# Eight slots for the experts' results, expert weights stored by blocks, and x turned earlier

## The chip, the cores and the metric

The kernel runs on one core of a Trainium2 chip. The metric is device time in microseconds, the median of several executions. TensorE (PE) multiplies, VectorE (DVE), ScalarE (ACT) and GpSimd (POOL) do the rest, SyncE (SP) mostly issues DMAs.

## What is computed

Four batches of 512 rows of 512 numbers pass through linear cross-attention over 1024 context rows and then a mixture of eight experts, two for each row. Cut to what matters:

```python
# x = x + attention(layernorm(x), ctx)
q = feature_map(query @ Wq.T);  gate = sigmoid(query @ Wg.T + bg)
k, v = split(kv @ Wkv.T);       k = feature_map(k)          # 16 heads of 32
attn = (q @ (k.T @ v)) / (q @ k.sum() + EPS)                # per head
out = (attn * gate) @ Wo.T
# x = x + ffn(layernorm(x))
w, sel = top_k(x @ Wr, 2);      w = softmax(w)
out = sum over the two chosen experts e of w_e * (x @ We[e] + be[e])
```

All products are of float32 accuracy. They are made of three products of fp32r halves: each operand is split in an upper half and the rest (high and low in the code), and high x high, high x low, low x high are summed.

## The kernel before

**Attention** goes batch by batch. `keys(b)` takes the eight context tiles: transpose (T c), K product, V product, and the kv sum (KV) of the tile before; between them stand the routing of the batch before (T z, L, K) and the transposes of this batch's x (T x 0 to 3). The order is written out by hand in the list KEYS, and every engine walks the same list with its own part: for a transpose TensorE turns the tile into PSUM, ACT copies the upper half (line 611), DVE subtracts to get the lower half (line 781). After V, ACT copies the product to SBUF (line 654), and KV of that tile waits for it. `queries(b)` follows: Q, gates, attention, output product, and the residual x2, which lies in the buffer `gate` (x2 is the same memory) and is stored to the output by SP (`store_x2`).

**Expert weights** are split on POOL beside attention: `cut_to_dram(e, h)` splits half an expert (lines 503 and 505) and stores both halves to the HBM buffer `we_halves` in one DMA (line 509). An expert's copy in SBUF needs the memory of attention's weights (R), so SP loads it back, 2 MB at once (`load_halves`, line 365), as these come free in the last batch: experts 1 to 3 during its keys and queries, 4 and 5 after the gates, 6 and 7 after the last output product. POOL issues in order; between the cuts it also makes rstd and shift of the layer norms (`scale`, lines 469 and 470), for which ACT waits, and scatters the normed rows into the experts' regions of the HBM buffer `xs` (line 462). At the start it fills the heads of these regions with zeros, in as many DMAs as there are result slots (YS).

**The expert stage** works on tiles of 128 rows of one expert, 39 in all: 17 with the full tiles of the first three batches, which begin while the last batch is routed, then 22 for the rest. Four of these 22 are empty here. For each tile m: `load_tile` brings the rows; TensorE turns them (line 1188), ACT and DVE split them (lines 698 and 785); TensorE multiplies (lines 1121 to 1123); ACT writes the expert's bias times the row's weight into the result slot `y_sb[m % YS]` (line 724) and first waits until the add of tile m - YS, which used this slot, has landed; DVE adds the weighted product to it (line 1072); POOL adds the result's rows to the output in HBM by an indirect accumulating DMA (`add_rows`, line 579). Two adds that may meet in a row of the output must not be in flight together. Two tiles of one expert have no row in common. So the first tile of an expert waits for the landing of the add just before it where their rows may meet (`tile_alone`), and the first and second tile wait for all older ones still in flight (`tile_early`); a third tile waits for nothing. At tile 17 (M0) all adds before have to be down. With YS slots, up to YS - 1 adds can be older and in flight, and the code names each of them:

```python
elif m >= 1:
    alone = pool.value_load(tile_alone[0:1, m:m + 1], ...)
    early_ = pool.value_load(tile_early[0:1, m:m + 1], ...)
    pool.wait_ge(added[(m - 1) % YS], alone + 16 * ((m - 1) // YS + 1))
    for d in range(2, min(m, YS - 1) + 1):
        pool.wait_ge(added[(m - d) % YS], early_ + 16 * ((m - d) // YS + 1))
```

The first tile of the stage is turned at 390.7 us, between the last output products. Which expert has how many tiles follows from the inputs; in the order of tiles it is 3, 2, 3, 2, 2, 2, 3 (experts 0 to 6), the four empty ones, then 1, 2, 2, 3, 2, 3, 2, 3 (experts 0 to 7).

Of the kernel before, what the change touches and what calls it, by code (L numbers as in the profile page):

```python
# [5 lines left out]
F32 = mybir.dt.float32  # L6
# [8 lines left out]
P = 128  # L15
# [5 lines left out]
def xattn_moe_kernel(nc, x, ctx_in, wq_t, wg_t, bg, wkv_t, wo_t, wr, we, be, out):  # L21
# [34 lines left out]
    XS, YS = 4, 4  # L56

    xs_dram = nc.dram_tensor("xs", [(E + 1) * ROWS, W], F32, kind="Internal").ap()
    wx_dram = nc.dram_tensor("we_halves", [E, P, 2 * KT * D], F32, kind="Internal").ap()
# [3 lines left out]
    with ExitStack() as stack:  # L63
# [43 lines left out]
        y_sb = [khat[:, 0, :], khat[:, 1, :], expk[:, 0, :], expk[:, 1, :]]  # L107
# [7 lines left out]
        x2 = gate  # L115
        w_raw += [gate[:, :, :], qhat[:, :, :], w_raw[0]]
# [25 lines left out]
        gap = sb("gap", [P, 1])  # L142
        egap = sb("egap", [P, 1])
        total = sb("total", [P, 1])
# [12 lines left out]
        w_sel = sb("w_sel", [P, 2 * YS])  # L157
        out_idx = sb("out_idx", [P, 2 * YS], U32)
# [37 lines left out]
        e_high, we_ready = sem("e_high"), sem("we_ready")  # L196
# [109 lines left out]
        def _(sp):  # L306
# [64 lines left out]
            sp.wait_ge(wx_stored, 16 * 2 * (E - 1))  # L371
# [14 lines left out]
            load_halves(7)  # L386
# [12 lines left out]
        def _(pool):  # L399
# [96 lines left out]
            def cut_to_dram(e, h):  # L496
# [4 lines left out]
                pool.wait_ge(wx_stored, 16 * u)  # L501
# [7 lines left out]
                pool.dma_start(wx_dram[bass.ds(e, 1), :, :].rearrange("x p (a k d) -> p (x a) k d", a=2, k=KT)[:, :, ks, :],  # L509
                               aux[:, :, :].rearrange("p (a k) d -> p a k d", a=2).bitcast(F32)).then_inc(wx_stored, 16)  # L510
# [50 lines left out]
            def add_rows(m):  # L561
# [17 lines left out]
                nc.gpsimd.indirect_dma_start(out=out_rows[:, :], out_offset=bass.IndirectOffsetOnAxis(ap=out_idx[:, m % (2 * YS):m % (2 * YS) + 1], axis=0),  # L579
# [12 lines left out]
        def _(act):  # L592
# [100 lines left out]
            def high_m(m, slot):  # L693
                act.wait_ge(MOE["t_m"], mth(m))
                if m == 0:
                    act.wait_ge(wx_stored, 16 * 2 * (E - 1))
# [16 lines left out]
            def gate_bias(m):  # L713
# [581 lines left out]
```

## Time and profile before

| | us |
|---|---|
| median of 3 runs | 560.09 (558.15 to 564.46) |
| the profiled execution | 555.62 |
| its span in the trace | 554.1 |
| TensorE busy | 517.2 (93%) |
| DVE / ACT / POOL busy | 304.5 / 208.8 / 203.4 |

Attention takes the first 390 us, the expert stage the rest. A trace row has a start, a duration, the engine (SPq, ACTq, POOLq: its instruction queue), the line, the tiles (out<-in), and in brackets how long the engine was idle before and what ended that. TensorE's granted clock is 0.993 of full over the span.

### The profile page before, as it was taken

To read this page: it belongs to the slowest core of one execution; us is meant where nothing else is said; L and a number is where in the kernel's file an instruction comes from. 1 tells how busy PE (TensorE), PEld (TensorE's weight loads), DVE (VectorE), ACT (ScalarE), POOL (GpSimd) and SP (SyncE) were. 2 spreads that over 40 slices of the span, in tenths; PEclk is the share of its full clock that TensorE was granted. 3 is DMA by queue.
4 is the path that set the end of the run, shared out by engine and by line. 5 is a ranking of instruction groups with operands and counts; after the bars stand their busy time and mean duration, and the time that the engine had idled before them with its cause. 6 is when DMAs were issued, how large, how long until landed. Compare 5 with 4: busy or idle time off the path is not lost.

```text
span 554.1 us, 12191 instructions
## 1 busy us (share of the span) xinstructions
PE 517.2 (93%) x4080; PEld 420.1 (76%) x4080; DVE 304.5 (55%) x918; ACT 208.8 (38%) x372; POOL 203.4 (37%) x221
## 2 busy tenths in 40 slices
PE   6999999999999999999999999999988878997990
PEld 4777788788878888777888877788866666886880
DVE  4483248547524764753585475378577674453540
ACT  6455432443443234344324344432343233332430
POOL 4443246502654040364404036100133563444453
PEclk9999999999999999999999999999999999999997
DMA  8922943652445135244513412697998788746855
GB/s 254 401 86 75 294 152 115 231 188 72 149 167 188 41 126 180 78 152 159 182 46 129 176 55 105 228 351 277 342 334 190 177 161 166 155 96 121 166 73 68
DMA packets 34361, 92.93 MB, mean 168 GB/s; under 512 B 4544, under 2 KB 4544, under 8 KB 33280
## 3 DMA queue, kind: packets, MB, share of 16 engines
q0 software_dynamic: 14960, 42.56, 28.9%
q1 hardware_dynamic: 18048, 47.22, 24.9%
q10 hardware_dynamic: 1296, 2.40, 1.3%
q8 instruction: 35, 0.57, 0.4%
q14 instruction: 22, 0.18, 0.1%
HBM read 53.81 MB, written 40.18 MB: 170 GB/s over the span
## 4 chain that ended last, share of the span: by engine, by line
PE 58%; DMA 14%; issue 6%; POOL 3%; POOLq 3%; DVE 2%; ACT 1%; ACTq 1%; DVEq 0%
PE pj L1121 16%; PE pj L1123 16%; PE pj L1122 16%; DMA out_dram<-khat,out_idx 6%; DMA out_dram<-buf,out_idx 5%; PE tp L1113 5%; PE pj L1208 2%; POOL aux L505 1%; PE kvb L1180 1%; DMA wraw<-in_L_ffn_We_dram 1%; DMA we_halves<-aux 1%; POOLq L574 1%; PE pj L1130 1%; POOLq L573 1%; PE tp L1188 1%
## 5 line engine op out<-in xcount | busy, mean ns | idle before, releaser
L1121 PE MATMUL pj<-R 128*128 128x512 f32 x448 | 184.2, 411 | 5.7 <-DVE R L781 5.0
L1123 PE MATMUL pj<-R 128*128 128x512 f32 x448 | 176.2, 393 | 0.0
L1122 PE MATMUL pj<-R 128*128 128x512 f32 x448 | 175.4, 392 | 0.0
L1121 PEld LDWEIGHTS pj<-R 128*128 128x128 f32 x448 | 84.7, 189 | 23.2 <-DVE R L781 7.3
L1123 PEld LDWEIGHTS pj<-R 128*128 128x128 f32 x448 | 84.5, 189 | 19.0
L1122 PEld LDWEIGHTS pj<-R 128*128 128x128 f32 x448 | 84.9, 189 | 15.1
L1121 PE MATMUL pj<-R,aux 128*128 x156 | 64.8, 416 | 12.0 <-DVE aux L785 10.2
L1123 PE MATMUL pj<-R,aux 128*128 x156 | 61.4, 393 | 0.0
L1122 PE MATMUL pj<-R,aux 128*128 x156 | 60.8, 390 | 0.0
L781 DVE TENSOR_TENSOR R<-tp,R 128x512 fp32r<-128x512 f32 x64 | 43.8, 684 | 23.2 <-ACT R L611 23.2
L846 DVE SCALAR_TENSOR_TENSOR khat<-buf,khat 128x512 f32<-128x512 f32 x32 | 24.2, 756 | 51.6 <-ACT buf L650 50.9
L469 POOL TENSOR_TENSOR rstd<-rstd,mhalf 128x1 f32<-128x1 f32 (+1 forms) x20 | 13.4, 670 | 100.4 <-DVE rstd L799 100.3
L579 POOL DMA_INDIRECT out_dram<-khat,out_idx x20 | 31.4, 1571 | 39.9 <-issue 15.2
L1121 PEld LDWEIGHTS pj<-R,aux 128*128 128x128 f32 x156 | 29.3, 188 | 19.9 <-issue 15.0
L579 POOL DMA_INDIRECT out_dram<-buf,out_idx x19 | 29.6, 1560 | 39.7 <-DMA out_dram<-khat,out_idx 13.6
L611 ACT CAST R<-tp 128x512 fp32r<-128x512 f32 x64 | 37.6, 588 | 16.9 <-PE tp L1113 16.6
L462 POOL DMA_INDIRECT xs<-normed,xidx x16 | 18.5, 1155 | 67.2 <-DVE xidx L832 64.1
L654 ACT COPY buf<-pj 128x512 f32<-128x512 f32 x32 | 18.8, 587 | 51.3 <-PE pj L1123 51.3
L647 ACT ACTIVATE khat<-pj 128x512 f32<-128x512 f32 x32 | 19.1, 597 | 47.6 <-PE pj L1123 47.6
L505 POOL TENSOR_TENSOR aux<-wraw,aux 128x1024 fp32r<-128x1024 f32 x14 | 35.8, 2554 | 1.2
L1123 PEld LDWEIGHTS pj<-R,aux 128*128 128x128 f32 x156 | 29.3, 188 | 6.5
L1122 PEld LDWEIGHTS pj<-R,aux 128*128 128x128 f32 x156 | 29.4, 188 | 5.1
(196 smaller groups left out, 699.2 us busy)
## 6 DMA issues: line engine op xcount, KB each, us to landing
we_halves<-aux POOLq DMA_DIRECT2D x14, 1024.0 KB, 4.9
R<-we_halves SPq DMA_DIRECT2D x7, 2048.0 KB, 9.5
buf<-xs SPq DMA_DIRECT2D x34, 264.0 KB, 3.7
buf<-in_ctx_dram SPq DMA_DIRECT2D x15, 512.0 KB, 3.6
wraw<-in_L_ffn_We_dram POOLq DMA_DIRECT2D x14, 512.0 KB, 6.6
wraw<-in_x_dram SPq DMA_DIRECT2D x4, 1024.0 KB, 8.8
out_dram<-gate SPq DMA_DIRECT2D x4, 1024.0 KB, 5.2
xs<-zeros POOLq DMA_DIRECT2D x4, 594.0 KB, 9.7
```

The lines of the kernel that those rows point to most:

```text
L462: nc.gpsimd.indirect_dma_start(out=xs_dram[:, :], out_offset=bass.IndirectOffsetOnAxis(ap=xidx[:, t, j:j + 1], axis=0), in_=rows[t], in_of ...
L505: nc.gpsimd.tensor_tensor(aux[:, 2:4, :], e_raw[:, ks, :], aux[:, 0:2, :].bitcast(F32), ALU.subtract).then_inc(wx_low, 1)
L579: nc.gpsimd.indirect_dma_start(out=out_rows[:, :], out_offset=bass.IndirectOffsetOnAxis(ap=out_idx[:, m % (2 * YS):m % (2 * YS) + 1], axis=0),
L611: nc.scalar.copy(dst, src).then_inc(SEMS["h_" + kind], 1)
L647: nc.scalar.activation(khat[:, i % 2, :], pj_bank("expk", i)[:, :], ACT.Relu)
L654: nc.scalar.copy(vones[:, i % 2, :, 0:HD], pj_bank("v_copied", i)[:, :].rearrange("p (g c) -> p g c", g=HEADS)).then_inc(SEMS["v_copied"], 1)
L781: nc.vector.tensor_tensor(lo, tp_bank("l_" + kind, i)[:, :, :], hi.bitcast(F32), ALU.subtract).then_inc(SEMS["l_" + kind], 1)
L846: nc.vector.scalar_tensor_tensor(khat[:, i % 2, :], expk[:, i % 2, :], 1.0, khat[:, i % 2, :], ALU.min, ALU.add).then_inc(SEMS["khat"], 1)
L1113: last = nc.tensor.transpose(bank[:, k, :], src[:, k * P:(k + 1) * P], ident[:, :])
L1121: nc.tensor.matmul(bank[:, :], s_hi(k), m_hi(k), start=(k == 0), stop=False)
L1122: nc.tensor.matmul(bank[:, :], s_hi(k), m_lo(k), start=False, stop=False)
L1123: last = nc.tensor.matmul(bank[:, :], s_lo(k), m_hi(k), start=False, stop=(k == KT - 1))
```

## The change

- YS goes from 4 to 8. The four new slots are the four tiles of x2 (the buffer `gate`); ACT waits for the store of the last batch's x2 before it writes the first of them (tile 4). The rings of weights and indices have YS + 2 = 10 columns in place of 2 YS = 8.
- `we_halves` has the shape [expert, 8 blocks, partition, 512] in place of [expert, partition, 8 x 512]. A store of halves becomes two DMAs, a load reads eight pieces of 2 KB for each partition in place of one of 16 KB.
- Expert 7 is loaded in two halves: the first right after expert 3's load, the second after expert 6's.
- In KEYS the transpose of x's tile 3 (T x 3) goes from behind V of the last context tile to ahead of it.
- TensorE starts with a product on zeros (128 columns) and makes another (256 columns) after its first transposes.
- gap, egap and total share one tile.

```diff
-    XS, YS = 4, 4
+    XS, YS = 4, 8
-    wx_dram = nc.dram_tensor("we_halves", [E, P, 2 * KT * D], F32, kind="Internal").ap()
+    wx_dram = nc.dram_tensor("we_halves", [E, 2 * KT, P, D], F32, kind="Internal").ap()
-        y_sb = [khat[:, 0, :], khat[:, 1, :], expk[:, 0, :], expk[:, 1, :]]
+        y_sb = [khat[:, 0, :], khat[:, 1, :], expk[:, 0, :], expk[:, 1, :]] + [x2[:, t, :] for t in range(TT)]
...
-            KEYS += [("P", "k", i), ("T", "c", i + 1) if i + 1 < ST else ("T", "x", 2), ("P", "v", i)]
+            KEYS += [("P", "k", i)]
+            KEYS += [("T", "c", i + 1)] if i + 1 < ST else [("T", "x", 2), ("T", "x", 3)]
+            KEYS += [("P", "v", i)]
...
-            KEYS += [("T", "x", 3)] if i == ST - 1 else []
...
             def load_halves(e):
-                sp.wait_ge(wx_stored, 16 * 2 * e)
+                sp.wait_ge(wx_stored, 32 * 2 * e)
                 sp.wait_ge(we_ready, 16 * e)
-                sp.dma_start(R[:, 2 * e:2 * e + 2, :, :].rearrange("p a k d -> p (a k d)").bitcast(F32), wx_dram[e, :, :]).then_inc(we_ready, 16)
+                sp.dma_start(R[:, 2 * e:2 * e + 2, :, :].rearrange("p a k d -> p (a k) d").bitcast(F32),
+                             wx_dram[e, :, :, :].rearrange("a p d -> p a d")).then_inc(we_ready, 16)
+
+            def load_half(e, a):
+                if a:
+                    sp.wait_ge(we_ready, 16 * e)
+                    sp.wait_ge(half_loaded, 16)
+                sp.dma_start(R[:, 2 * e + a, :, :].bitcast(F32),
+                             wx_dram[e, a * KT:(a + 1) * KT, :, :].rearrange("k p d -> p k d")).then_inc(we_ready if a else half_loaded, 16)
...
             load_halves(3)
+            load_half(7, 0)
...
             load_halves(6)
-            load_halves(7)
+            load_half(7, 1)
...
-                pool.dma_start(wx_dram[bass.ds(e, 1), :, :].rearrange("x p (a k d) -> p (x a) k d", a=2, k=KT)[:, :, ks, :],
-                               aux[:, :, :].rearrange("p (a k) d -> p a k d", a=2).bitcast(F32)).then_inc(wx_stored, 16)
+                for a in range(2):
+                    pool.dma_start(wx_dram[bass.ds(e, 1), a * KT + 2 * h:a * KT + 2 * h + 2, :, :].rearrange("x k p d -> p (x k) d"),
+                                   aux[:, 2 * a:2 * a + 2, :].bitcast(F32)).then_inc(wx_stored, 16)
...
                 act.wait_ge(paid, m + 1)
+                if m == YS - TT:
+                    act.wait_ge(x2_stored, 16 * B + 16)
                 if m >= YS:
                     act.wait_ge(added[m % YS], 16 * (m // YS + 1))
...
-            pe.wait_ge(pool_step, 3)
...
+            def idle_product(n):
+                nc.tensor.matmul(kvb[1][:, 0:n], zeros[:, 0:P], zeros[:, 0:n], start=True, stop=True)
+
+            pe.wait_ge(zeroed, 1)
+            idle_product(P)
+            pe.wait_ge(pool_step, 3)
             pe.wait_ge(ctx_first, 16)
             turn("c", 0, 0, ctx_raw[:, 0, 0, :])
+            idle_product(D // 2)
```

## Rows read from the trace of the kernel before

**Rows 1.** The page, busy time of the engines over the whole span.

```profile
PE 517.2 (93%) x4080; PEld 420.1 (76%) x4080; DVE 304.5 (55%) x918; ACT 208.8 (38%) x372; POOL 203.4 (37%) x221
```

**Rows 2.** Table by windows: window, length, busy (instructions) by engine, clock, DMA, GB/s.

```profile
161.00:258.00 97.00, 95.98 (x864) 78.72 (x864) 53.42 (x168) 37.09 (x68) 33.19 (x34) 1.00 0.38 133
...
422.00:554.10 132.10, 108.01 (x536) 87.03 (x536) 63.49 (x200) 40.40 (x66) 64.08 (x44) 0.97 0.69 133
```

**Rows 3.** Chain of waits, 396 us to the end: shares; start, us, what.

```profile
by line: DMA out_dram<-khat,out_idx 21.1%; DMA out_dram<-buf,out_idx 19.3%; issue 11.7%; PE pj L1121 6.8%; PE pj L1123 6.5%; PE pj L1122 6.3%; POOLq L574 3.3%; POOLq L573 2.8%; PE tp L1188 2.5%; POOL out_dram L579 1.9%; DVE buf L1072 1.4%; 
...
455.99 4.86 DMA out_dram<-buf,out_idx
461.10 0.51 issue
```

**Rows 4.** Waits of ACT from 400 us, of TensorE 430 to 535: us, times, longest.

```profile
ACT khat L724 <- DMA out_dram<-khat,out_idx: 30.9, 12, 5.1
ACT buf L724 <- DMA out_dram<-buf,out_idx: 28.9, 13, 4.6
...
PE pj L1121 <- DVE aux L785: 10.2, 8, 2.4
```

**Rows 5.** POOL's adds, line 579: timeline, then what ended its idle time.

```profile
422.20 1.55 POOL L579 DMA_INDIRECT out_dram<-buf,out_idx  x1 [9.70 <-DVE xidx L832]
...
461.81 1.55 POOL L579 DMA_INDIRECT out_dram<-khat,out_idx  x1 [4.26 <-DMA out_dram<-buf,out_idx]
...
546.44 1.55 POOL L579 DMA_INDIRECT out_dram<-buf,out_idx  x1 [0.92 <-DMA out_dram<-khat,out_idx]
...
  DMA out_dram<-khat,out_idx: 21.0, 8
  DMA out_dram<-buf,out_idx: 19.3, 8
```

**Rows 6.** Timeline of DVE: the results of tiles 2, 3 and 38.

```profile
408.08 0.75 DVE L1072 SCALAR_TENSOR_TENSOR buf<-pj,w_sel,buf 128x512 f32<-128x512 f32 x1 [0.91 <-ACT buf L724]
412.21 0.75 DVE L1072 SCALAR_TENSOR_TENSOR buf<-pj,w_sel,buf 128x512 f32<-128x512 f32 x1 [0.26 <-PE pj L1123]
...
542.06 0.75 DVE L1072 SCALAR_TENSOR_TENSOR buf<-pj,w_sel,buf 128x512 f32<-128x512 f32 x1 [3.12 <-ACT buf L724]
```

**Rows 7.** DMA issues 396 to 422, then 470 to 530: count, KB, us to landing.

```profile
R<-we_halves SPq DMA_DIRECT2D x2, 2048.0 KB, 11.2
out_dram<-khat,out_idx POOLq DMA_INDIRECT x2, 9.7
out_dram<-buf,out_idx POOLq DMA_INDIRECT x1, 10.3
...
out_dram<-buf,out_idx POOLq DMA_INDIRECT x10, 4.8
```

**Rows 8.** The same: stores of halves 105 to 119 us, then of the page.

```profile
we_halves<-aux POOLq DMA_DIRECT2D x1, 1024.0 KB, 6.4
...
we_halves<-aux POOLq DMA_DIRECT2D x14, 1024.0 KB, 4.9
```

**Rows 9.** Timeline of POOL in batch 0.

```profile
52.22 2.48 POOL L529 DMA_DIRECT2D xs<-zeros  x4
...
87.44 0.68 POOL L509 DMA_DIRECT2D we_halves<-aux  x1 [0.81 <-POOL aux L505]
```

**Rows 10.** Timeline of ACT and TensorE at batch 0's output products.

```profile
99.07 0.82 ACT L621 ACTIVATE normed<-gate,shift,rstd 128x512 f32<-128x512 f32 x1 [4.92 <-POOL shift L470]
...
101.14 0.50 PE L1121 MATMUL pj<-R 128*128 128x512 f32 x1 [0.51 <-DVE R L781]
```

**Rows 11.** Timeline at the end of a batch's keys.

```profile
256.08 0.60 PE L1113 MATMUL tp<-ident,num 128*128 128x128 f32 x4
256.28 0.59 ACT L654 COPY buf<-pj 128x512 f32<-128x512 f32 x1 [1.63 <-PE pj L1123]
...
258.14 0.50 PE L1121 MATMUL pj<-R 128*128 128x512 f32 x1 [0.66 <-DVE R L781]
```

**Rows 12.** Timeline of TensorE at the start, first K product of context tile 1.

```profile
14.96 0.50 PE L1121 MATMUL pj<-R 128*128 128x512 f32 x1 [0.50 <-DVE R L781]
```

More of the change, by code:

```diff
@@ L141, in xattn_moe_kernel @@
         top = sb("top", [P, E])
-        gap = sb("gap", [P, 1])
-        egap = sb("egap", [P, 1])
-        total = sb("total", [P, 1])
+        odds = sb("odds", [P, 3])
+        gap, egap, total = [odds[:, i:i + 1] for i in range(3)]
         idx8 = sb("idx8", [P, E], U32)
@@ L156, in xattn_moe_kernel @@
         xidx = sb("xidx", [P, TT, 2], U32)
-        w_sel = sb("w_sel", [P, 2 * YS])
-        out_idx = sb("out_idx", [P, 2 * YS], U32)
+        w_sel = sb("w_sel", [P, YS + 2])
+        out_idx = sb("out_idx", [P, YS + 2], U32)
         used = sb("used", [P, 1 + E])
@@ L195, in xattn_moe_kernel @@
         w_high, w_low = sem("w_high"), sem("w_low")
-        e_high, we_ready = sem("e_high"), sem("we_ready")
+        e_high, we_ready, half_loaded = sem("e_high"), sem("we_ready"), sem("half_loaded")
         first_loaded = [sem(f"first_loaded{k}") for k in range(KT)]
@@ L370, in _ @@
             load_halves(2)
-            sp.wait_ge(wx_stored, 16 * 2 * (E - 1))
+            sp.wait_ge(wx_stored, 32 * 2 * (E - 1))
             sp.dma_start(be_all[:, 0:4, :], be[0:4, :].rearrange("(a e) d -> a e d", a=1).broadcast_to((P, 4, D))).then_inc(be_loaded, 16)
@@ L500, in cut_to_dram @@
                 pool.wait_ge(e_loaded[h], 16 * e)
-                pool.wait_ge(wx_stored, 16 * u)
+                pool.wait_ge(wx_stored, 32 * u)
                 passed()
@@ L578, in add_rows @@
                 passed()
-                nc.gpsimd.indirect_dma_start(out=out_rows[:, :], out_offset=bass.IndirectOffsetOnAxis(ap=out_idx[:, m % (2 * YS):m % (2 * YS) + 1], axis=0),
+                nc.gpsimd.indirect_dma_start(out=out_rows[:, :], out_offset=bass.IndirectOffsetOnAxis(ap=out_idx[:, m % (YS + 2):m % (YS + 2) + 1], axis=0),
                                              in_=y_sb[slot], in_offset=None, bounds_check=B * L - 1, oob_is_err=False, compute_op=ALU.add).then_inc(added[slot], 16)
@@ L695, in high_m @@
                 if m == 0:
-                    act.wait_ge(wx_stored, 16 * 2 * (E - 1))
+                    act.wait_ge(wx_stored, 32 * 2 * (E - 1))
                 act.wait_ge(MOE["m_done"], mth(m - 2))
@@ L724, in gate_bias @@
                 nc.scalar.activation(y_sb[m % YS], be_all[:, bass.ds(e, 1), :].rearrange("p a d -> p (a d)"), ACT.Identity,
-                                     scale=w_sel[:, m % (2 * YS):m % (2 * YS) + 1]).then_inc(bias_gated, 1)
+                                     scale=w_sel[:, m % (YS + 2):m % (YS + 2) + 1]).then_inc(bias_gated, 1)
             bias_in(TT - 1)
@@ L919, in pay @@
                 e = dve.value_load(tile_expert[0:1, m:m + 1], min_val=0, max_val=E - 1)
-                n = m % (2 * YS)
+                n = m % (YS + 2)
                 row = xs_raw[:, m % XS, :]
@@ L1071, in copy_y @@
                 dve.wait_ge(bias_gated, m + 1)
-                nc.vector.scalar_tensor_tensor(y_sb[m % YS], pj[m % 2][:, :], w_sel[:, m % (2 * YS):m % (2 * YS) + 1], y_sb[m % YS],
+                nc.vector.scalar_tensor_tensor(y_sb[m % YS], pj[m % 2][:, :], w_sel[:, m % (YS + 2):m % (YS + 2) + 1], y_sb[m % YS],
                                                ALU.mult, ALU.add).then_inc(MOE["y_copied"], 1)
```

## The prediction

> **What bounds the kernel now.** The page comes first: TensorE is busy 93% of the span [rows 1]. That says "TensorE-bound", and it is an average over two unlike stages. The table by windows separates them [rows 2]: from 161 to 258 us TensorE is busy 95.98 of 97 us, but from 422 us to the end only 108.01 of 132.10 us. So the first 390 us, attention, go at TensorE's pace, and the last 132 us need another reason.
>
> The chain of waits of the last stretch names it [rows 3]: 40% of that stretch is the landing of two kinds of transfer, the accumulating stores `out_dram<-khat` and `out_dram<-buf`, the adds of line 579. ACT's waits seem to tell why: line 724, which prepares a result slot, waited 30.9 + 28.9 us for such landings [rows 4], since slot m % 4 is free only when add m-4 has landed. TensorE idles behind it, 10.2 us in 8 waits after 430 us [rows 4]. That is the wait which eight slots take away.
>
> But does the end hang on it? For that one compares when a result is there (end of DVE line 1072) with when its add starts on POOL. Result 3 is complete at 412.21 + 0.75 = 412.96 us [rows 6] and its add starts at 422.20 [rows 5]. Result 38, the last: 542.06 + 0.75 = 542.81 [rows 6] against 546.44 [rows 5]. Over the 36 adds from the fourth on, of which these are the first and the last, I find a finished result that waited 3.6 to 13.1 us for its add. The adds never wait for results; they wait for each other: the first tile of an expert waits until the previous expert's last add landed (line 575), the second until all older ones have (line 577). The rows show it: the add of 461.81 starts 0.96 us after the landing of the add of 455.99 (455.99 + 4.86 = 460.85) [rows 3, 5], and the next of the same expert follows as soon as POOL has issued this one, 1.55 us [rows 5] and 0.35 more. So from 422.20 us to the end the adds are a closed chain, through landings of about 5 us and issues, and TensorE, ACT and DVE run beside it with 3.6 us in hand or more.
>
> **Part 1, eight slots.** ACT's 59.8 us of waiting for landings goes, TensorE catches up its 10.2 us of idle time [rows 4], and the last product ends some 10 us earlier. None of it is on the adds' chain: which add waits for which is set by the experts' borders, and these stay. Worth to the end: 0. What is late next is the adds' chain, as before. What the part does put on that chain: an add now names up to seven earlier slots instead of three. The wait that ends last comes first in the list, so the four more stand behind it. From that landing (460.85) to the last sequencer instruction ahead of the start (461.10) pass 0.25 us for three instructions [rows 3], 0.08 us each. Four more waits are two instructions if two waits share one (0.16 us), four if not (0.33 us). The answer on line 579 names 8 + 8 adds that a landing released [rows 5]; with four more whose gap is put down otherwise I count 20 links. I take 0.15 us: 20 x 0.15 = +3.0 us; bounds 0 (hidden) and 20 x 0.33 = +6.6. The other adds have these waits under the 1.55 us of the issue before. The first zero fill is cut into eight stores instead of four, counted in part 3. Slots 4 to 7 lie in x2, whose store is issued before the first add and takes some 6 us; the first result that goes there is number 4, after 412.96, so that wait costs 0.
>
> **Part 2, the halves in HBM by blocks.** An expert's 2 MB load was 16 KB in one piece for each partition; now it is eight rows of 2 KB. The first half of expert 7 goes ahead of the last batch's queries, so 1 MB less lies behind expert 6's load. The place where this meets the end is the head of the chain: between 396 and 422 us two such loads take 11.2 us each and the adds beside them 9.7 and 10.3 us [rows 7], while in the quiet stretch from 470 us an add lands in 4.8 us [rows 7]. Add 3 starts at 422.20 [rows 5] because add 2 landed only after these 10.3 us. What would an add take beside 2 KB pieces? The nearest row is the 1 MB store at 111.9 us, beside x and context loads whose rows are 2 KB: 6.4 us, against 4.9 alone [rows 8], 1.5 more. So 4.9 + 1.5 = 6.4 us for add 2, and the chain starts 10.3 - 6.4 = 3.9 us sooner. Value -3.9; bounds 0 (no relief) and -5.5 (4.8 us, as in quiet). Result 3 (412.96) and the scatter's inputs are there in time, so the gain isn't stopped on the way. Everything behind it moves with it. The loads themselves grow a little; expert 6 is due first at tile 14, at about 449 us, and is there by some 410 to 420: hidden, and even 15 us a load would be.
>
> **Part 3, each store of halves in two.** 14 stores of 1 MB become 28 of 0.5 MB, all on POOL; one issue takes 0.68 us there, 0.61 until the next begins [rows 9]. In batches 1 to 3 POOL waits for DVE (up to 36.9 us at line 469), so they are hidden. In batch 0 they aren't: POOL's work from 52 to 99 us is one chain, the rstd at its end comes late, ACT waited 4.92 us for it and TensorE then 0.51 us at 101.14 [rows 10]. On that path lie: the second issue after the store of 74.78, ahead of the loads of 75.70 (+0.6); the landing of the store of 87.44 before the copy of 92.45 (+0.25 to 0.6); the second issue before rstd at 98.08 (+0.6); and four more zero fills of 0.62 us each (52.22, 2.48 us for four [rows 9]), which stand ahead of a store that waits for the fills' traffic anyway until 70.2 us, +0 to 0.6. Together 1.5 to 2.4: value +1.8 us, and TensorE has no later slack in this stage to win it back. Bounds +0.9 and +2.5.
>
> I take the two halves' fixed parts to run side by side; the third rival has them one behind the other. The Trainium skill (DMA: Bandwidth & Descriptors, section "Anatomy of one DMA — SWDGE (gpsimd) path") gives a GpSimd DMA about 2.0 us that don't shrink with its size, which speaks against cutting one in two. The 4.9 us of [rows 8] for 1 MB agree with such a part; whether two of them overlap, no row here shows.
>
> **Part 4, x's fourth tile turned before the last V product.** At the end of each batch's keys TensorE waits for x's last lower half: 0.66 us at 258.14 [rows 11], and 0.66 to 0.71 in the other batches. Moved ahead, its copies run under the V product. But its 0.44 us of transposes also covered ACT's copy of V: that copy starts at 256.28 and takes 0.59, ends 256.87 [rows 11], and would now come 0.79 us after V's end with only 0.37 us of kv work in between: a new gap of 0.42 us before the last kv sum. Per batch 258.14 - 256.08 = 2.06 us before, 0.79 + 0.03 + 0.43 + 0.44 = 1.69 after: -0.37, four times -1.5 us. Bounds 0 and -2.7 (the gaps whole).
>
> **Part 5, idle products at the start.** The first products go at half the pace of the later ones. Two products on zeros could bring the clock up earlier. But TensorE then waits 0.50 us at 14.96 for DVE [rows 12], which follows ACT's copies of the weights, and these follow their DMA. Faster products only make that wait longer: 0. They run while TensorE waits for its first inputs: cost 0.
>
> The merged small tiles and the shorter ring of ten columns add no instruction: 0.
>
> **Sum.** +3.0 - 3.9 + 1.8 - 1.5 = -0.6 us. The profiled execution took 555.62 us (span 554.1), so 555.0 in its terms; the median of the runs shown is 560.09, 4.5 higher, so 559.5.
>
> **Rivals.**
> - *No relief at the head (0.15)*: adds are slow there because of all the bytes, not the pieces: -0.6 + 3.9 = +3.3, 563.4 us. For: DMA is also busy with 2 KB and 2112-byte rows; against: 6.4 us in [rows 8] under like load.
> - *Full relief (0.15)*: adds 1 and 2 also start 0.9 us after their results (result 2: 408.08 + 0.75 [rows 6]): 408.83 + 0.9 + 4.8 + 0.95 = 415.5, 6.7 us sooner: -3.4, 556.7 us.
> - *Fixed parts in series (0.08)*: 1 MB takes 2.6 us at the 401 GB/s of the page's busiest slice, so of a store's 4.9 us [rows 8] 2.3 aren't data. Twice on batch 0's path that is 4.6 in place of 0.3: +4.3, together +3.7: 563.8 us. Against: POOL issues the second half 0.6 us behind the first and waits for neither.
> - *The slots pay in full (0.07)*: the end follows TensorE, 10.2 us less: 549.3. For: the page's 93% and ACT's waits. Against: results that lie finished for 3.6 us and more.
> - *Slower (0.07)*: the waits' list. If every extra wait also takes its own register work, 0.16 us each, a link costs 0.64 and 20 links 12.8: 0.3 - 3.9 + 12.8 = +9.2, 569 us. It decides from 0.46 us a link. Against: 0.08 us an instruction in [rows 3].
> - My forecast holds the rest, 0.48, with -4 to +3 us.
>
> **How the numbers follow.** Within 1% (5.6 us), about what can be told from no change, lie the forecast, no relief, the series and most of full relief. Faster by over 1%: the slots in full 0.07, and 0.08 from full relief together with hidden waits. Slower: the list 0.07, and 0.04 where no relief meets the upper bound of the waits. The range runs from full relief with its lower bounds (553) to no relief with costly waits (565).
>
> **What would show it.** In the new profile: ACT's waits for `out_dram` landings nearly gone; TensorE's last product about 10 us earlier in the stretch, with the end of the kernel not following; results finished over 10 us before their adds at the end; add 2 landing in 6 to 7 us and the fourth add near 418 us; the start 1.1 instead of 0.95 us behind a landing; TensorE's wait near 101 us grown to about 2.3; no wait on line 781 at the keys' ends and a new one of 0.4 before kv. I am wrong if the end moves with TensorE, or if the adds' landings in the quiet stretch change.

## The result, and the profile after

| | us |
|---|---|
| changed kernel, median of 4 | 565.74 (561.69 to 569.73) |
| kernel before, on the same chip | 559.12 (556.54 to 564.46) |
| ratio | 1.0099, interval 1.0059 to 1.0139 |
| again, median of 6, beside 11 of the kernel before | 565.59; ratio 1.0122 (1.0084 to 1.0160) |

The forecast was 559.5 us, within 553 to 565. The kernel became slower by 1%: 5.5 us by the first ratio, 6.8 by the second. Its profiled execution has a span of 565.0 us against 554.1, which is 2.0% and more than either ratio. So not all that the two traces differ in is the change, and the experiments have to say what is.

**Where the slots were to help, they did what they do.** First the waits of ACT at the slots (line 737 now) from 400 us: of the 59.8 us of [rows 4] for landings nothing is left here (a second profile of the changed kernel has 13.7 us, behind results that lie still further ahead).

```profile
ACT khat L737 <- issue: 3.4, 4, 2.2
ACT buf L737 <- DVE out_idx L937: 1.9, 2, 1.3
ACT gate L737 <- issue: 1.5, 4, 0.7
```

Then the ends of DVE and of POOL in the timeline. The last result is complete at 544.96 + 0.75 = 545.71 us and its add starts 11.65 us later; in [rows 5, 6] it was 3.63. The adds still follow each other's landings.

```profile
544.96 0.75 DVE L1085 SCALAR_TENSOR_TENSOR gate<-pj,w_sel,gate 128x512 f32<-128x512 f32 x1 [1.97 <-PE pj L1135]
...
552.12 1.55 POOL L590 DMA_INDIRECT out_dram<-gate,out_idx  x1 [2.09 <-DMA out_dram<-buf,out_idx]
...
557.36 1.55 POOL L590 DMA_INDIRECT out_dram<-gate,out_idx  x1 [1.11 <-DMA out_dram<-gate,out_idx]
```

**The head of the chain.** Adds 2 and 3 in POOL's timeline. In the trace add 2 lands 6.53 us after its start, at 425.42 (10.3 us in [rows 7]), and add 3 follows it by 1.03 us. Attention ended 8.4 us later than before, add 3 starts only 4.25 us later than the 422.20 of [rows 5].

```profile
418.89 1.56 POOL L590 DMA_INDIRECT out_dram<-buf,out_idx  x1 [2.76 <-issue]
426.45 1.55 POOL L590 DMA_INDIRECT out_dram<-buf,out_idx  x1 [6.01 <-issue]
```

**The new stall lies in batch 0.** Where TensorE waited 0.51 us [rows 10], it now waits 5.61, because ACT waited 9.63 us for POOL's shift (4.92 before), which POOL makes right behind a late rstd:

```profile
103.72 0.59 POOL L479 TENSOR_TENSOR rstd<-rstd,mhalf 128x1 f32<-128x1 f32 x1
104.62 0.81 ACT L632 ACTIVATE normed<-gate,shift,rstd 128x512 f32<-128x512 f32 x1 [9.63 <-POOL shift L480]
...
106.68 0.79 PE L1133 MATMUL pj<-R 128*128 128x512 f32 x1 [5.61 <-DVE R L794]
```

and the granted clock of TensorE falls during that wait, at 103.5 us, and is back at 110.3. The line of the page gives it in tenths for 40 slices of 14 us; the eighth, 99 to 113 us, is the one. First the kernel before:

```profile
PEclk9999999999999999999999999999999999999997
```

then the changed one, and below it its table by windows (window, length, busy by engine, clock, DMA share, GB/s). Half clock is the lower of the two levels, 1.2 of 2.4 GHz. The kernel before has 1.00 in both windows.

```profile
PEclk9999999799999999999999999999999899999985
```

```profile
99.00:104.00 5.00, 2.07 (x12) 1.50 (x10) 0.40 (x3) 0.00 (x0) 4.24 (x5) 0.95 0.24 92
104.00:110.00 6.00, 3.32 (x8) 2.64 (x9) 2.98 (x7) 2.92 (x5) 1.97 (x6) 0.50 0.59 186
```

Following POOL back from there one comes to the first store of expert halves. POOL's timeline before, after the fills of [rows 9]:

```profile
59.19 0.72 POOL L509 DMA_DIRECT2D we_halves<-aux  x1 [0.64 <-POOL aux L505]
70.34 1.03 POOL L503 CAST aux<-wraw 128x1024 fp32r<-128x1024 f32 x1 [10.43 <-issue]
...
74.78 0.68 POOL L509 DMA_DIRECT2D we_halves<-aux  x1 [0.60 <-POOL aux L505]
```

and after:

```profile
53.38 4.38 POOL L540 DMA_DIRECT2D xs<-zeros  x8
57.76 1.06 POOL L513 CAST aux<-wraw 128x1024 fp32r<-128x1024 f32 x1
...
61.92 1.50 POOL L520 DMA_DIRECT2D we_halves<-aux  x2 [0.63 <-POOL aux L515]
75.44 1.04 POOL L513 CAST aux<-wraw 128x1024 fp32r<-128x1024 f32 x1 [12.02 <-issue]
79.55 0.73 POOL L520 DMA_DIRECT2D we_halves<-aux  x1 [0.59 <-POOL aux L515]
```

The second cut begins when the first store has landed: at 75.44 instead of 70.34 us. These 5.1 us are nearly all of the 5.6 us by which rstd is late at 103.72 (98.08 before).

**Keys.** The new order shows as forecast: no wait of 0.66 us behind the kv sums, but one of 0.38 ahead of the last (0.42 forecast).

```profile
264.95 0.59 ACT L665 COPY buf<-pj 128x512 f32<-128x512 f32 x1 [1.58 <-PE pj L1135]
...
265.68 0.46 PE L1192 MATMUL kvb<-buf,khat 128*32 128x33 f32 x32 [0.38 <-ACT buf L665]
```

**Two more differences, and a suspicion.** In the middle of the keys of batches 1 to 3 TensorE now has a wait that the trace of the kernel before doesn't have, and the whole batch gets some 0.7 us longer by what stands around it:

```profile
236.50 0.50 PE L1192 MATMUL kvb<-buf,khat 128*32 128x33 f32 x25 [0.47 <-issue]
```

And at 432.73 us DVE had stood still for 3.46 us before it took logits whose product was done at 428.75. The results of tiles 6 to 9 come late after it, and the adds 9 to 11 start 2.4 to 3.0 us behind their results: for these three the results are the bound. From add 8 to add 12 pass 18.3 us here and 15.2 in the mean of the other profiles: about 3 us of the end.

```profile
432.73 0.17 DVE L817 COPY lg<-pj 128x8 f32<-128x8 f32 x1 [3.46 <-remote]
...
456.18 1.58 POOL L590 DMA_INDIRECT out_dram<-khat,out_idx  x1 [3.99 <-DMA out_dram<-khat,out_idx]
```

At the start the first profile of the changed kernel differs too: its keys of batch 0 end 1.6 us later than before.

The theory at this point: the two stores or the eight fills make batch 0 late (one had been priced, +1.8 us for both), the list of waits is dearer than 3.0 us, and the last two differences may be of one execution only. The rival: eight slots themselves disturb the early tiles.

### The profile page after: what moved, and what is told of

The parts are those of the page before. It is cut to its first block, busy times and chain, and to the rows that moved or that the text cites. A ratio compares the mean times of both kernels' runs of the same rounds, so it can differ in the third digit from the quotient of the medians.

```text
span 565.0 us, 12322 instructions
## 1 busy us (share of the span) xinstructions
PE 522.4 (92%) x4084; PEld 423.2 (75%) x4084; DVE 307.2 (54%) x918; ACT 211.4 (37%) x372; POOL 214.2 (38%) x239
## 4 chain that ended last, share of the span: by engine, by line
PE 73%; DMA 5%; issue 4%; POOL 2%; DVE 2%; another core or an unknown queue 1%; POOLq 1%; ACT 0%; DVEq 0%
PE pj L1133 21%; PE pj L1135 20%; PE pj L1134 19%; PE tp L1125 5%; PE tp L1200 3%; PE pj L1220 2%; PE kvb L1192 2%; POOL aux L515 1%; DMA wraw<-in_L_ffn_We_dram 1%; PE pj L1142 1%; DMA we_halves<-aux 1%; DMA out_dram<-khat,out_idx 1%; DMA out_dram<-buf,out_idx 1%; DMA out_dram<-gate,out_idx 1%
## 5 line engine op out<-in xcount | busy, mean ns | idle before, releaser
L1134 PEld LDWEIGHTS pj<-R 128*128 128x128 f32 x448 | 85.5, 191 | 15.3
L479 POOL TENSOR_TENSOR rstd<-rstd,mhalf 128x1 f32<-128x1 f32 (+1 forms) x20 | 13.3, 666 | 100.4 <-DVE rstd L812 100.3
L709 ACT CAST aux<-tp 128x512 fp32r<-128x512 f32 x39 | 22.8, 584 | 60.3 <-PE tp L1200 52.2
L590 POOL DMA_INDIRECT out_dram<-gate,out_idx x19 | 29.7, 1565 | 37.5 <-issue 24.5
L472 POOL DMA_INDIRECT xs<-normed,xidx x16 | 17.1, 1068 | 64.8 <-DVE xidx L845 61.8
L1133 PEld LDWEIGHTS pj<-R,aux 128*128 128x128 f32 x156 | 29.7, 190 | 15.3 <-issue 10.2
L1135 PEld LDWEIGHTS pj<-R,aux 128*128 128x128 f32 x156 | 29.5, 189 | 6.7
L916 DVE SCALAR_TENSOR_TENSOR qhat<-buf,qhat 128x512 f32<-128x512 f32 x16 | 17.4, 1086 | 30.9 <-ACT buf L690 30.8
```

What stands on the lines that cost most here:

```text
L709: nc.scalar.copy(xsT_hi[:, slot, :, :], tp[slot][:, :, :]).then_inc(MOE["h_m"], 1)
L1133: nc.tensor.matmul(bank[:, :], s_hi(k), m_hi(k), start=(k == 0), stop=False)
L1134: nc.tensor.matmul(bank[:, :], s_hi(k), m_lo(k), start=False, stop=False)
L1135: last = nc.tensor.matmul(bank[:, :], s_lo(k), m_hi(k), start=False, stop=(k == KT - 1))
```

## The experiments

All ratios are to the kernel before, run beside them; in brackets stands the 95% interval.

### One part at a time

**Eight slots alone**, with four fills as before; the counters of the four new slots are raised by small stores into a spare buffer:

```diff
-    XS, YS = 4, 4
+    XS, YS = 4, 8
...
+            for s in range(FILLS, YS):
+                pool.dma_start(spare[s:s + 1, :], zeros[0:1, :]).then_inc(added[s], 16)
```

> The kernel before with eight result slots (and the waits of the adds that belong to them), but four zero fills as before; the four new slots' counters are raised by four 2 KB stores into a spare buffer, issued where GpSimd idles. Theory A (waits' list only, adds' chain closed): ACT's waits for out_dram landings go, the end does not follow TensorE; the chain from add 12 to add 38 is 2 to 4 us longer than the 84.6 us of before, the time +2 to +4 us, ratio 1.004 to 1.007. Rival B (the slots themselves disturb DVE and TensorE in tiles 6 to 11, so results are late there): as in the changed kernel adds 9 to 11 start within 3 us of their results, add 9 is 3 us or more later against attention's end, ratio 1.010 or more. Rival C (slots pay): ratio under 0.995.

Measured: 562.47 us, ratio 1.0065 (1.0030 to 1.0101). The end doesn't follow TensorE: the last result lies finished for 13.3 us. The adds 9 to 11 start 4.5 us or more behind their results, so rival B falls; C too. From add 12 to add 38 pass 88.8 us, 4.1 more than before and at the upper edge of theory A. The run has the long list of waits as well, so it doesn't price the slots without it.

**The list of waits alone**, with four slots; the new waits are satisfied long before:

```diff
-                    for d in range(2, min(m, YS - 1) + 1):
+                    for d in range(2, min(m, 2 * YS - 1) + 1):
```

> The kernel before, four slots, with only the list of waits ahead of an add made as long as in the changed kernel: up to seven waits instead of three, all the new ones satisfied long before. Theory A (each further wait costs about 0.08 us where a landing releases the add): landing to start 1.05 to 1.25 us instead of 0.95, from add 12 to 38 +2 to +3 us, time +2 to +4 us, ratio 1.004 to 1.007. Rival: the waits are hidden and the longer chain of the changed kernel comes from slower landings: add 12 to 38 within 1 us of 84.6, ratio 1.000 +- 0.002.

Measured: 563.46 us, ratio 1.0044 (1.0011 to 1.0077). The chain of waits around the add of tile 12 shows the price in single instructions (start, us, what). The landing ends at 460.11 + 4.94 = 465.05 us:

```profile
460.11 4.94 DMA out_dram<-buf,out_idx
465.06 0.03 issue
465.08 0.03 POOLq L577
...
465.32 0.02 POOLq L577
465.33 0.04 issue
465.38 0.04 POOLq L413
...
465.51 0.51 issue
466.02 0.29 POOLq L573
...
467.63 0.51 issue
```

From the landing to the start at 466.23 pass 1.18 us instead of 0.96 [rows 3, 5]. Between the landing and the start line 577 has four instructions here and one in the kernel before. And the add of tile 13 starts 2.12 us behind it instead of 1.90: its instructions begin at 466.02, when POOL's sequencer has handed over the add before, and end only at 467.63 + 0.51. They are not hidden under the 1.55 us of that add. So adds pay 0.22 us also where no landing releases them. Not all do: the adds of tiles 4, 6, 7 and 8 stand behind two scatters of rows each and follow the add before by 4.45 to 4.47 us in this run, as in the kernel before (4.45 or 4.46). From add 12 to add 38 pass 89.8 us, 5.1 more than before, where theory A had said 2 to 3; the ratio lies where it had said.

**The layout alone**: blocks of 2 KB rows, two stores, expert 7 in two halves; four slots, four fills (the diff is that of `we_halves`, `load_half` and line 520 above).

> The kernel before with the halves in HBM by blocks alone: stores of halves in two, loads in 2 KB rows, the first half of expert 7 early; four slots, four zero fills, keys' order as before. Theory A (two stores cost on the path of batch 0, the head of the adds' chain gains): TensorE's gap near 101 us grows from 0.5 to 4 us or more with a fallen clock behind it if the two stores are its cause, add 2 lands in 6 to 7 us instead of 10.3, last add -4 against attention's end; sum +1 to +3 us. Rival B (the eight zero fills cause the stall in batch 0): the gap stays under 1.5 us and the time falls by 2 to 4 us, ratio 0.993 to 0.997.

Measured: 558.18 us, ratio 0.9973 (0.9939 to 1.0007). Theory A's gain at the head came (add 2 lands in 7.3 us); its stall did not: TensorE waits 1.85 and 1.24 us in batch 0, at full clock. Rival B had said under 1.5 us. The two stores cost little. Where the queues are quiet, the first of two lands in 3.2 us and the second in 4.7, or 5.4 from the first one's issue, where 1 MB in one took 4.85: 0.55 us for the pair. So the fixed parts do run side by side. By the Trainium skill (DMA: Bandwidth & Descriptors, section "Anatomy of one DMA — SWDGE (gpsimd) path"), 2.0 us plus size over 436 GB/s, half a megabyte is estimated at 3.2 us. The trace agrees for the first of the two; for 1 MB the same working gives an estimate of 4.4 us, where the trace has 4.85.

**The eight fills alone**:

```diff
-            QP = P // YS
+            QP = P // (2 * YS)
...
-            for s in range(YS):
+            for s in range(2 * YS):
```

> The kernel before with the first zero fill cut into eight stores instead of four and nothing else. Rival B of the run before (fills cause the stall in batch 0): the cut of halves that ended at 74.8 us ends 3 us or more later, TensorE's gap near 101 us is 3 us or more, clock falls behind it, time +4 to +6 us, ratio 1.007 to 1.011. Theory A (the two stores cause it): the cut ends within 1.5 us of before, gap under 1.5 us, ratio 1.000 to 1.003.

Measured: 563.99 us, ratio 1.0085 (1.0053 to 1.0117): rival B of the layout's run. The stall of the changed kernel is there, with stores of 1 MB and four slots:

```profile
52.50 4.37 POOL L529 DMA_DIRECT2D xs<-zeros  x8
...
61.05 0.73 POOL L509 DMA_DIRECT2D we_halves<-aux  x1 [0.65 <-POOL aux L505]
74.82 1.04 POOL L503 CAST aux<-wraw 128x1024 fp32r<-128x1024 f32 x1 [13.04 <-issue]
...
105.09 0.79 PE L1122 MATMUL pj<-R 128*128 128x512 f32 x1 [4.61 <-DVE R L782]
```

The busy share of the DMA engines from 52 to 77 us, in 40 slices, shows why the store waits. With eight fills:

```profile
DMA  5599788999999999997979898777743332100000
```

before:

```profile
DMA  9699978799999999999998999952000000000069
```

In the traces the same 2.43 MB of zeros are 576 pieces of 4224 bytes with four fills, 227 ns each, 131 us of engine time; with eight they are 512 such pieces at 269 ns and 128 of 2112 bytes at 157 ns, 158 us. That is 1.7 us more on 16 engines, the four more issues take 1.9 us (4.37 against 2.48), and the last pieces trickle out on a part of the engines: the digits sink, from 68 us on for good, and reach 0 at 74, where before they stay at 9 until 68 and reach 0 at 70.

### Repeats

**The kernel before, unchanged.**

> The kernel before, unchanged: a second profile. Theory A (the new waits in the middle of the keys, 0.5 us at the kv product of block 4 and 0.7 us at the key product before it in batches 1 to 3, and a spread of 2 us in when batch 0's first store of halves lands, come and go from one execution to the next): this profile shows the 0.5 us gaps near 134, 231 and 328 us as all changed kernels do, the first store may land at 70 to 73 us. Rival B (they come with any change of the program): no such gaps, store at 70.2 us, span 554 us. Ratio 1.000 either way.

Measured: ratio 1.0009 (0.9974 to 1.0043). No 0.5 us waits in the keys, the second cut at 71.0 us, span 556.0 us: rival B, as far as one profile can say. **The changed kernel, unchanged:**

> The changed kernel, unchanged, a second profile. Theory A (what its first profile shows in batch 0 belongs to the program, what it shows at 432.7 us and in the middle of the keys does not): the first stores of halves land again at 71 to 73 and 74 to 76 us, TensorE's gap at its output products is 4 to 6 us with a fallen clock behind it; VectorE does not wait over 3 us for logits near 432 us and the adds 9 to 11 start 4 us or more behind their results; ratio 1.007 to 1.013. Rival B (the late results of tiles 6 to 9 come with the changed program): the wait near 432 us and adds 9 to 11 within 3 us of their results show again. Rival C (batch 0's stall was a chance too): gap under 3 us, ratio under 1.006.

Measured: ratio 1.0122. The stall of batch 0 is there again, with clocks of 0.81 and 0.59 in the two windows:

```profile
105.10 0.80 PE L1133 MATMUL pj<-R 128*128 128x512 f32 x1 [5.16 <-DVE R L794]
```

DVE's wait at 432 us is not. From add 3 on results lie 7.1 to 23.6 us ahead of their adds, 17.1 at the last one, and yet the last add starts at 556.47 us. So the late results of tiles 6 to 9 belong to one execution, and are not needed for the loss.

The wait in the middle of the keys follows neither kernel: it is in all four profiles of the first group of runs (slots, waits, layout, fills) and in all four of the third (the changed kernel with early fills, the kernel with 4 KB rows and early fills, that with late loads, the idle products), and in none of the second (the repeat of the kernel before, keys, early fills, 4 KB rows alone) nor in any later one. It is in the first profile of the changed kernel and not in that of the kernel before: about 2 us of their difference that are not the change. What sets it stays open. The 1.6 us at the start are 0.5 in the second profile of the changed kernel; over all profiles the end of batch 0's keys spreads from -0.4 to +2.3 us, whatever the edit.

### The other parts

**Keys' order alone** (the diff of KEYS above):

> The kernel before with only the last-but-one order change: x's fourth tile turned ahead of the last V product of each batch. Theory A (0.66 us wait replaced by one of 0.38 ahead of the last kv sum): each batch's end of keys 0.3 to 0.4 us shorter, four times, ratio 0.997 to 0.999. Rival B (the order is neutral or slower by 0.3 us a batch, as the sum over whole batches in the changed kernel seems to say): ratio 1.000 to 1.003.

Measured: 558.83 us, ratio 0.9997 (0.9965 to 1.0030), too coarse to tell the theories apart. In the trace each batch's keys are 0.33, 0.27, 0.27 and 0.27 us shorter: -1.1 us, at the lower edge of theory A.

**Idle products alone**:

> The kernel before with only the two idle products at the start of TensorE. Theory A (the start is set by DMA, ScalarE and VectorE, and by when the clock rises, which the two products do not move): clock rises at 10.3 to 11.4 us, end of the first keys within 1 us of before, ratio 0.999 to 1.001. Rival B (the clock comes up earlier and the start gains): rise before 9.5 us, keys' end 1 us or more earlier, ratio 0.997 to 0.999. Rival C (they delay the first products, as the 1.05 us at the changed kernel's start would say): ratio 1.001 to 1.003.

Measured: ratio 0.9980 (0.9943 to 1.0017). The end of batch 0's keys is 0.9 us later than in the first profile of the kernel before; kernels that leave the start as it was lie between -0.4 and +2.3. The clock rises at 12.6 us, where theory A had said 10.3 to 11.4; in the other profiles it rises between 9.7 and 13.5. No effect can be told.

### The fills out of the way

The queues stand almost idle from 30 to 40 us, so the fills can go ahead of POOL's wait for the last weights:

```diff
+            for s in range(YS):
+                pool.dma_start(fronts[s * QP:(s + 1) * QP, :, :], ...)
             pool.wait_ge(w_low, 5 * KT)
             load_expert(1, 0)
             load_expert(1, 1)
```

In the kernel before:

> The kernel before with its four zero fills issued about 11 us earlier, ahead of GpSimd's wait for the last of the weights, where the queues stand nearly idle (2% busy from 30 to 40 us). Theory A (the fills' traffic ahead of the first store of halves makes batch 0's chain late): the first store lands within 6 us of its issue, before 65 us instead of 70 to 72; TensorE's gap near 101 us and any fallen clock behind it go; time -0.5 to -4 us, ratio 0.993 to 0.999. Rival B (the fills meet the context loads at 40 us and TensorE waits there): new gap before 60 us, ratio 1.000 or more.

Measured: 554.97 us, ratio 0.9968 (0.9941 to 0.9995), theory A: the second cut begins at 65.0 us, and TensorE has no wait near 101. There is no new one before 60 us either. In the changed kernel:

> The changed kernel with its eight zero fills issued about 11 us earlier, ahead of GpSimd's wait for the last weights; nothing else. Theory A (the eight fills ahead of the first store are the stall of batch 0): first store lands before 67 us instead of 71.8 and 75.3, TensorE's gap near 107 us of 5.6 us and the fallen clock behind it gone, time 6 to 9 us under the changed kernel, ratio to the kernel before 0.996 to 1.002. Rival B (the doubled stores hold batch 0 up as well): a gap of 2 us or more stays, ratio 1.003 to 1.007. If the late results of tiles 6 to 9 (VectorE held 3.5 us at 432.7 us by logits that were done at 428.8) belong to the program, they show again, with adds 9 to 11 within 3 us of their results; if they came by chance, not.

Measured: 558.10 us, ratio 0.9972 (0.9946 to 0.9998): theory A, and the loss of 1% is gone, with eight slots, doubled stores and eight fills all in place. Its POOL in the timeline:

```profile
38.72 4.42 POOL L537 DMA_DIRECT2D xs<-zeros  x8
...
62.19 1.46 POOL L520 DMA_DIRECT2D we_halves<-aux  x2 [0.64 <-POOL aux L515]
67.10 1.04 POOL L513 CAST aux<-wraw 128x1024 fp32r<-128x1024 f32 x1 [3.44 <-issue]
```

In its table by windows TensorE is busy through the stretch of the stall, at full clock:

```profile
99.00:104.00 5.00, 5.00 (x26) 4.14 (x25) 3.44 (x11) 1.52 (x3) 1.47 (x4) 1.00 0.00 0
```

Batch 0 over all profiles, where lateness is how much longer the stretch from its queries to its last output product takes than in the first profile of the kernel before (0.7 us are added where x's fourth tile is turned early, since its transposes then lie ahead of the stretch):

| fills | second cut begins | TensorE's longest wait | lateness, us |
|---|---|---|---|
| four, one store (7 profiles) | 70.3 to 72.3 | 0.5 to 1.2, but 3.3 in two | 0 to 0.9, 4.5 and 4.8 in two; mean 1.6 |
| four, two stores (1) | 72.7 | 1.9 | 3.0 |
| eight (3) | 73.6 to 75.4 | 4.6 to 5.6 | 6.0 to 6.4 |
| early, four or eight (6) | 64.7 to 67.1 | none over 0.6 | -1.2 to +0.3 |

So the eight fills cost about 4.5 us against the mean of the first row (6.1 - 1.6). Of their lateness 1.7 to 2.4 us are the clock: in the five profiles where TensorE waits 3.3 to 5.6 us at this place, products behind the wait run at the lower level, and the lateness goes on growing by 1.6 to 2.4 us after it. Four fills can come to this too: two of the seven profiles show it, those of the slots alone and of the keys' order, and neither of the two of the kernel before.

### What the first adds gain from

**Blocks of 4 KB rows with one store**: `we_halves` is [expert, 4 blocks, partition, 1024] and is read back in rows of 4 KB, the rest of the layout as in the change. The diff against the changed kernel, cut to the store:

```diff
-                for a in range(2):
-                    pool.dma_start(wx_dram[bass.ds(e, 1), a * KT + 2 * h:a * KT + 2 * h + 2, :, :]...
+                pool.dma_start(wx_dram[bass.ds(e, 1), :, :, :].rearrange("x (a g) p c -> p (x a) g c", a=2)[:, :, h, :],
+                               aux[:, :, :].rearrange("p (a k) d -> p a (k d)", a=2).bitcast(F32)).then_inc(wx_stored, 16)
```

> The kernel before with halves in HBM by blocks of 4 KB rows: one store of 1 MB as before, loads in 4 KB rows, first half of expert 7 early. Theory A (relief at the head of the adds' chain comes from what the loads' pieces leave to the adds, and the second store costs about 1 us in batch 0): add 2 lands in 7 to 8 us, batch 0 as in the kernel before (gap 0.5 to 3 us), time -2.5 to -4 us, ratio 0.993 to 0.996, a little under the layout with two stores (0.997). Rival B (only 2 KB pieces relieve): add 2 lands in 9.5 to 10.5 us, ratio 0.999 to 1.001.

Measured: 554.91 us, ratio 0.9959 (0.9928 to 0.9990), and add 2 lands in 7.7 us: theory A. **With the early fills and the keys' order on top**, four slots:

> What paid, without the eight slots: blocks of 4 KB rows with one store of 1 MB (ratio 0.996), zero fills, four, issued ahead of the wait for the last weights (0.997), x's fourth tile turned ahead of the last V product (-0.3 us a batch by the trace); four result slots and the short list of waits. If the three add up: ratio 0.990 to 0.993, -4 to -5.5 us. If early fills and blocks free the same time: 0.994 to 0.996.

Measured: 556.57 us, ratio 0.9944 (0.9919 to 0.9969), the lesser of the two forecasts; add 2 takes 10.4 us here. **The loads of experts 6 and 7 moved behind those of tiles 10 and 12:**

> The kernel of the run before, with the load of expert 6 moved behind the loads of tiles 9 and 10 and the second half of expert 7 behind that of tile 12. Theory A (what slows adds 0 to 2 to 7 or 8 us is these loads): add 2 lands in 5 to 6 us, the fourth add 2 to 3 us earlier against the end of attention, one or two later adds 1 to 2 us slower; net 0 to -2 us against the run before. Rival B (the adds are slow by the store of the attention result and x's loads): add 2 lands in 7 us or more, net 0. If expert 6 comes too late for its tile, TensorE waits near 447 us: the end need not follow, since results lie 4 us ahead of their adds there.

Measured: 557.75 us, ratio 0.9964 (0.9935 to 0.9992). Adds 0 and 1 land in 4.8 us and add 2 in 6.4, so these loads are what slows them; but then adds 3 and 4 take 9.2 and 10.0 us, and the chain from the fourth add to the last takes 129.9 us, 6.9 more than in the run before. The gain is given back.

**2 KB against 4 KB rows**, both with early fills and the new order of keys, side by side:

> The changed kernel without its eight slots (four slots, short list of waits, four zero fills, these issued early, no idle products): halves by blocks of 2 KB rows with two stores, x's fourth tile turned early. Theory A (2 KB pieces give the adds at the head their relief, 3.6 us against attention's end in four profiles, and the second stores cost nothing now that batch 0's chain has slack): add 2 lands in 6.5 to 8 us, fourth add 3 to 4 us earlier against attention's end than in the kernel before, time 1 to 3 us under the kernel with 4 KB rows, ratio 0.988 to 0.993. Rival B (4 KB rows are as good, the head's 10.4 us there was one execution): same ratio as that one within 0.2%.

> The kernel with 4 KB rows, one store, four early zero fills and x's fourth tile turned early, unchanged, beside the one with 2 KB rows. Theory A: add 2 again near 10 us, fourth add within 1.5 us of the kernel before against attention's end, ratio 0.992 to 0.996. Rival B: add 2 lands in 7 to 8 us as in the kernel with 4 KB rows alone, ratio the same as with 2 KB rows.

Measured: 553.06 us, ratio 0.9916 (0.9885 to 0.9948) with 2 KB rows; 552.00 us, 0.9894 (0.9858 to 0.9930) with 4 KB rows. The intervals overlap: no difference can be told, and theory A of both runs falls: the 2 KB kernel is not 1 to 3 us faster, and in the one with 4 KB rows add 2 lands in 7.8 us. That kernel is the one that measured 0.9944 above, unchanged; its two intervals only just overlap, so its gain is 0.6% to 1.1%. Against attention's end the fourth add starts 2.8 to 4.2 us earlier in five profiles with 2 KB rows (mean 3.5), and 1.7 earlier, 0.7 later and 1.4 earlier in three with 4 KB rows; in eight profiles of the old layout it moves by -1.6 to +1.8 (mean 0.0). By the traces 2 KB rows relieve the head more. What wins it back with 4 KB rows the runs don't show; in the two profiles taken side by side the keys of batch 0 end 2 us earlier with 4 KB rows, which may be the spread of the start. Both kernels beat the kernel before and, by the two ratios to it (they were not run beside each other), the changed one by about 2%.

## Why the prediction was wrong

**The bound and the slots (0): right.** ACT's waits for landings went or lost their weight, the last result lies 11.7 to 17.1 us ahead of its add, the end didn't follow. The slots pay nothing, neither together with the rest nor alone. The "3.6 us in hand" are less than they look: where a result was the bound (adds 10 and 11 of the first profile), its add started 2.4 us behind it, so of 3.6 us only 1.2 were slack.

**The head (-3.9): right in size.** Measured against attention's end it is -3.5 us on average over five profiles. Add 2 landed in 6.5 us against 6.4 forecast, but that is the lowest of the five (up to 8.0, mean 7.2), and with the old layout it takes 7.6 to 11.8 us (mean 9.7 in eight profiles), so the 10.3 of [rows 7] was no fixed price either. These means differ by 2.5 us only. The adds ahead of it, which the forecast left out, land sooner too (add 1 in 8.6 us instead of 11.5, by the means). So that a difference of two single landings came this near is partly luck.

**The keys (-1.5): nearly right,** -1.1, and both waits as described. **The idle products (0)**: nothing to be told from 0.

**The list of waits (+3.0): the price of a link too low, one sentence of it false, the total open between 2.5 and 5.2.** The chain from the fourth add to the last takes 123.0 to 126.8 us in eleven profiles with the short list (mean 124.9; the run with late loads is left out), and 127.9 to 132.0 in five with the long one (mean 130.1): +5.2 us. Late results add about 3 to one of the five, which leaves +4.6. From add 12 on alone, behind the scatters and the late results, the same profiles give 88.4 to 89.8 us (mean 88.9) against 83.9 to 87.3 (mean 85.5): +3.5 us. By the ratios of the two single runs it is +2.5 and +3.6 us, with intervals of 0.6 to 4.3 and 1.7 to 5.7, which hold the 3.0. Forecast were 20 links at 0.15 us. A link costs 0.22, since four more waits are three more instructions and not two, and "the other adds have these waits under the 1.55 us of the issue before" is wrong: the sequencer starts on them only when it has handed over the add before, so the next add is 0.22 us later as well, and the next link waits for that one's landing.

**Batch 0 (+1.8): here the forecast fell.** The term was worked out from the doubled stores. In the one profile that has them with four fills they are worth 1.4 us (3.0 - 1.6, the table), or 2.6 against the five undisturbed profiles of the first row; beside eight fills they add nothing clear (6.0 and 6.3 with them, 6.0 without). That part was near. The step that failed is "four more zero fills ... stand ahead of a store that waits for the fills' traffic anyway until 70.2 us, +0 to 0.6". The store does wait for that traffic, but the landing moves with what stands ahead of it: the four issues (1.9 us) come before POOL's own cut, and smaller fills keep the queues busy longer (1.7 us and a thin tail). Measured: +4.5 us, of which 1.7 to 2.4 came by the fallen clock, which no term held. The stretch was known to be a chain without slack; that a late arrival there can cost more than itself wasn't asked.

The sum with the measured terms is 5.2 - 3.5 + 4.5 - 1.1 = +5.1 us, and +3.4 with 3.5 for the list, against +5.5 and +6.8 by the ratios: 0.4 to 3.4 us stay unexplained. By the ratios of the parts alone it closes better: +0.65% (slots with their waits) + 0.85% (fills) - 0.27% (layout) - 0.03% (keys) - 0.20% (idle products) = +1.0%, where 0.99 and 1.22% were measured. But each part is known to 0.3 or 0.4% only, the sum to about 0.8% (the root of the five squares), so that it closes so well is partly luck. Of the rivals, "slower by the list of waits" named the right sign and part of the cause at a price three times too high per link. "Fixed parts in series" had said 4.6 us for a doubled store, where 0.55 were measured. None named the fills.

## What to carry to other kernels

Before giving a stage more buffers, look at the distance between the end of a result and the start of what takes it away, and subtract what that distance is where the result is the bound (here 3.6 and 2.4 us): where something is left every time, buffers buy nothing, and the names they add to a list of waits are paid again at most of the instructions behind the list. Ask what else the constant sets: here the number of slots also cut an unrelated fill into smaller DMAs, in the one stretch that had no slack. Traffic ahead of a store that the path waits for belongs where the queues are idle; 11 us earlier its cost doesn't show, and it paid 0.3% in the kernel before and the whole 1% in the changed one.

And take a second profile of both kernels before explaining a difference of 2 or 3 us between two traces: here two such differences, of about 2 and 3 us, did not belong to the change.

## What the hardware showed that had not been expected

- The same zeros in eight DMAs of 16 partitions took 158 us of DMA engine time, in four of 32 partitions 131 us. By count (128 single rows of 2112 bytes in eight fills, none in four), each of the 16 engines is left with one single row per small fill, where the larger fills have only pairs of 4224 bytes; and a pair took 269 ns instead of 227.
- Waits of TensorE of 3.3 to 5.6 us in batch 0 (five profiles) came with 1.6 to 2.4 us lost at the lower clock level behind them; waits of 0.5 to 1.9 us there (six profiles), with none.
- Four waits more on GpSimd's sequencer cost an indirect DMA 0.22 us, also where it follows another without a landing between; where two scatters stood between, they cost nothing (4.45 us from add to add either way).
- A wait of 0.5 us in the middle of each batch's keys, present in all profiles of one group of runs and absent in all of another, on the same chip, whatever the change.
